# One attention layer inside a fused kernel: transposes alternate with attend products, a score product moves to the end of the step, normalising goes to three engines

## The reference

```python
scores = einsum('bqhd,bkhd->bhqk', q, k) / sqrt(32)      # 16 heads of 32
probs  = softmax(where(causal, scores, min))
attn   = einsum('bhqk,bkhd->bqhd', probs, v) @ Wo.T
mod    = 0.1 * tanh(attn @ A)
h      = rmsnorm(x, ln2_w)
gate   = silu(h @ W_in.T + mod * (h @ A) @ B)
out    = x + gate * (h @ W_up.T) @ W_down.T
```

## Time and profile before

| | us |
|---|---|
| median of 3 runs (1060.45 to 1062.85) | 1061.8 |
| the profiled execution | 1061.96 |
| its span | 1059.8 |
| PE busy | 1033.5 (98%) |
| DVE busy | 722.4 (68%) |
| ACT busy | 589.6 (56%) |
| POOL busy | 252.1 (24%) |

### The profile page before, as it was taken

The page is one execution under the profiler, slowest core; times in us unless marked ns, Lnnn a source line. Parts: engine busy times, 40 slices in busy tenths (PEclk is TensorE's granted clock), DMA queues, the critical chain, the costliest instruction groups (busy, mean ns, idle before and its releaser), DMA issues.

```text
span 1059.8 us, 17623 instructions
## 1 busy us (share of the span) xinstructions
PE 1033.5 (98%) x5336; PEld 853.5 (81%) x5337; DVE 722.4 (68%) x1661; ACT 589.6 (56%) x1399; POOL 252.1 (24%) x252
## 2 busy tenths in 40 slices
PE   6999999999999999999999999999999999999998
PEld 6787878877888878878888888778888888788887
DVE  7766756996665559985665479966655599854443
ACT  4464546886434447875444368864344478753342
POOL 4536123641000115640000136410001155300000
PEclk9999999999999999999999999999999999999999
DMA  6534133443222416343322354432234253322221
GB/s 239 201 141 161 49 117 74 96 110 134 90 89 91 147 47 173 69 127 129 106 90 89 111 141 98 113 130 90 89 91 147 63 157 80 95 86 89 89 89 50
DMA packets 47084, 115.93 MB, mean 109 GB/s; under 512 B 6800, under 2 KB 6800, under 8 KB 46096
## 3 DMA queue, kind: packets, MB, share of 16 engines
q1 hardware_dynamic: 43968, 105.06, 33.2%
q0 software_dynamic: 3040, 9.96, 2.7%
HBM read 76.46 MB, written 13.37 MB: 85 GB/s over the span
## 4 chain that ended last, share of the span: by engine, by line
PE 86%; DVE 8%; issue 3%; DMA 1%; ACT 1%; SPq 0%; DVEq 0%; POOL 0%; POOLq 0%
PE bank L518 67%; PE bank L721 5%; PE bank L735 4%; DVE wr L1329 3%; PE bank L684 3%; DVE nb L1341 2%; PE bank L688 1%; PE bank L770 1%; DMA stack<-wr 1%; PE bank L574 1%; PE bank L589 1%; DVE big L1350 1%; PE bank L632 1%; SPq L312 0%; ACT wr L887 0%
## 5 line engine op out<-in xcount | busy, mean ns | idle before, releaser
L518 PE MATMUL bank<-hT,wr 128*128 128x512 f32 x1488 | 358.4, 390 | 0.0
L518 PEld LDWEIGHTS bank<-hT,wr 128*128 128x128 f32 x1488 | 278.8, 188 | 60.0 <-issue 1.3
L518 PE MATMUL bank<-wr,actr 128*128 128x512 f32 (+1 forms) x1224 | 303.1, 397 | 2.4 <-DVE actr L1311 1.5
L518 PEld LDWEIGHTS bank<-wr,actr 128*128 128x128 f32 x1224 | 228.8, 190 | 51.1 <-issue 3.3
L491 POOL TENSOR_SCALAR big<-big,rr 128x128 f32<-128x128 f32 (+1 forms) x128 | 138.9, 1094 | 131.7 <-DVE rr L1346 131.2
L1380 DVE SCALAR_TENSOR_TENSOR wr<-stream,lns,wr 128x256 fp32r<-128x256 f32 x256 | 121.7, 536 | 51.0 <-ACT wr L1006 51.0
L972 ACT ACTIVATE big<-bank,nb 128x512 f32<-128x512 f32 (+3 forms) x256 | 131.7, 527 | 27.9 <-DVE nb L1341 27.7
L430 POOL TENSOR_TENSOR wqs<-wstage,wqs 128x512 fp32r<-128x512 f32 x32 | 43.0, 1353 | 436.8 <-ACT wqs L887 435.4
L1329 DVE TENSOR_TENSOR wr<-bank,wr 128x512 fp32r<-128x512 f32 (+1 forms) x224 | 124.5, 600 | 22.2 <-ACT wr L887 22.2
L887 ACT ACTIVATE wr<-bank 128x512 fp32r<-128x512 f32 (+1 forms) x224 | 106.0, 538 | 52.9 <-PE bank L518 30.1
L887 ACT ACTIVATE actr<-act_sb 128x512 fp32r<-128x512 f32 x64 | 40.4, 632 | 145.7 <-DVE act_sb L1394 145.7
(11 more groups left out here) (180 smaller groups left out, 1039.6 us busy)
## 6 DMA issues: line engine op xcount, KB each, us to landing
stream<-in_wmlp SPq DMA_DIRECT2D x64, 512.0 KB, 4.0
stack<-wr SPq DMA_DIRECT2D x192, 128.0 KB, 2.3
stream<-in_wmlp SPq DMA_DIRECT2D x64, 256.0 KB, 2.7
big<-in_x SPq DMA_DIRECT2D x4, 1024.0 KB
big<-y_rows SPq DMA_DIRECT2D x4, 1024.0 KB, 5.5
residual<-big SPq DMA_DIRECT2D x4, 1024.0 KB
big<-residual SPq DMA_DIRECT2D x4, 1024.0 KB, 5.6
out<-big SPq DMA_DIRECT2D x3, 1024.0 KB, 4.5
```

The costliest lines, as they stand in the source:

```text
L518: mm = pe.matmul(dst, lhs(pl, k), rhs(pr, k), start=start and i == 0, stop=stop and i == n - 1, skip_group_check=skip)
```

## The change

Four things change. The order of the transposes is kt 2, 1, 3, 0, and ACT and DVE take the banks as 6, 5, 4. The four transposes of kt 0 alternate with the attend products of kt 2 and kt 1 of the head before. Of the scores, row tile 3 of head n+4 is done at the end of step n, tiles 2 and 0 between the transposes, row tile 1 between the attends; the half projection of the next step moves to the end of the step, ahead of the score product. Normalising: row tile 3 on DVE, 0 on ACT (after its first bank copy), 1 and 2 on POOL, whose weights now come ahead of its scalings. The values banks change places.

```diff
-VALUES, LOW_RANK = (4, 6), 5
+VALUES, LOW_RANK = (6, 4), 5
-NORM_DVE, NORM_POOL = (3, 1), (0, 2)
+NORM_DVE, NORM_ACT, NORM_POOL = 3, 0, (1, 2)
+TURNED_BANKS = ((6, 256, 1024), (5, 512, 512), (4, 512, 0))
+PART_OF = {2: 1, 1: 2, 3: 2, 0: 3}
...
@@ POOL @@
                     for j in range(QH):
+                        if j < 2 and q < NQ - 2:
+                            weights_high(b, q + 2, j)
+                            weights_low(b, q + 2, j)
                         if q < NQ - 1 or j < QH - 1:
                             normalise((b * NQ + q) * QH + j + 1)
-                        if j < 2 and q < NQ - 2:
-                            weights_high(b, q + 2, j)
-                            weights_low(b, q + 2, j)
@@ PE @@
+            def scores_last(n, par, loads, first=False):
                 pe.wait_ge(stk[par], loads)
                 if not first:
                     pe.wait_ge(exp_ok, n * 4 - 3)
+                score_rows(par, 3, True)
                 mask(0, 3 * P, 1)
+            def scores_middle(n, par, first=False):
                 if not first:
                     pe.wait_ge(exp_ok, n * 4 - 1)
+                score_rows(par, 2, True)
+                score_rows(par, 0, False)
                 mask(1, 2 * P, 2)
+            def scores_second(n, par, first=False):
                 if not first:
                     pe.wait_ge(exp_ok, n * 4)
+                score_rows(par, 1, True)
                 mask(2, P, 1)
...
+            def turn_tiles(n, par, kt, first=False):
+                if not first and kt != 3:
+                    pe.wait_ge(pt_lo, (n - 1) * 3 + PART_OF[kt])
+                for qt in range(kt, TT):
+                    turn(n, par, kt, qt)
...
@@ PE, head_step: the new step @@
                 if head < H - 1:
+                    wait_probs(n + 1)
+                    for kt in (2, 1, 3):
+                        turn_tiles(n + 1, other, kt)
                 if head < H - 3:
+                    scores_middle(n + 3, other)
+                if head < H - 1:
+                    pe.wait_ge(pt_lo, n * 3 + 3)
+                    turn(n + 1, other, 0, 0)
+                    attend(2, HI)
+                    turn(n + 1, other, 0, 1)
+                    attend(2, LO)
+                    turn(n + 1, other, 0, 2)
+                    attend(1, HI)
+                    turn(n + 1, other, 0, 3)
+                    attend(1, LO)
...
+                if head < H - 3:
+                    scores_second(n + 3, other)
+                attend(3, HI)
+                attend(3, LO)
...
+                attend(0, HI)
+                attend(0, LO).then_inc(pv_done, 1)
+                if head < H - 1:
+                    project_part(b, head + 1)
...
                     up_part(0, head - UP_FROM)
+                if head < H - 4:
+                    scores_last(n + 4, j % 2, stack_loads(b, head + 4))
@@ PE, prelude @@
+                wait_probs(b * H)
                 pe.wait_ge(vpa_ok, b + 1)
+                turn_tiles(b * H, 0, 2, first=True)
                 pe.wait_ge(ha_ok, b + 1)
-                turn_probs(b * H, 0, first=True, values_out=b + 1)
-                scores(b * H + 2, 0, b * (H // 2) * 48 + 96)
+                turn_tiles(b * H, 0, 1, first=True)
+                turn_tiles(b * H, 0, 3, first=True)
+                pe.wait_ge(vpb_ok, b + 1)
+                turn_tiles(b * H, 0, 0, first=True)
+                scores(b * H + 2, 0, stack_loads(b, 2))
                 project(b, 1, 1, half=0)
+                project_part(b, 0)
+                scores_last(b * H + 3, 1, stack_loads(b, 3))
@@ ACT @@
+            def normalise(n, par):
+                act.wait_ge(rr_ok, n + 1)
+                rows = prob_rows(par, NORM_ACT)
+                a.activation(rows, rows, ACT.Copy, scale=rr[:, par, NORM_ACT:NORM_ACT + 1]).then_inc(pn_act, 1)
...
-                for i, (bk, w, at) in enumerate(((4, 512, 0), (5, 512, 512), (6, 256, 1024))):
+                for i, (bk, w, at) in enumerate(TURNED_BANKS):
                     act.wait_ge(p_turned, n * 3 + i + 1)
                     copy(pts[:, j % 2, HI, at:at + w], bank[bk][:, 0:w]).then_inc(pt_hi, 1)
+                    if i == 0 and (q < NQ - 1 or j < QH - 1):
+                        normalise(n + 1, (j + 1) % 2)
```

More of the change, by code:

```diff
@@ L676, in project, with score_rows @@
                     mm.then_inc(qk_done, 1)
-            def scores(n, par, loads, first=False):
-                pe.wait_ge(stk[par], loads)
[L681 to L689, removed]
+            def score_rows(par, qt, start):
+                bk, col, _ = SCORE[qt]
+                w = P * (qt + 1)
+                pe.matmul(bank[bk][:, col:col + w], stack[:, par, 0, qt * P:qt * P + P],
+                          stack[:, par, 1, 0:w], start=start, stop=False, skip_group_check=True)
@@ L692, in scores, with mask @@
+            def mask(bk, at, n):
+                pe.matmul(bank[bk][:, at:at + P * n], identr[:, :], maskr[:, 0:P * n],
+                          start=False, stop=True, skip_group_check=True).then_inc(s_done, 1)
+            def scores_last(n, par, loads, first=False):
+                pe.wait_ge(stk[par], loads)
                 if not first:
                     pe.wait_ge(exp_ok, n * 4 - 3)
-                rows(3, True)
+                score_rows(par, 3, True)
                 mask(0, 3 * P, 1)
+            def scores_middle(n, par, first=False):
@@ L726, in attend @@
[L726 to L737, removed]
@@ L739, in head_step, with scores, turn @@
-            def head_step(b, q, j):
-                n = (b * NQ + q) * QH + j
-                head = q * QH + j
+            def scores(n, par, loads, first=False):
+                scores_last(n, par, loads, first)
+                scores_middle(n, par, first)
+                scores_second(n, par, first)
+            def turn(n, par, kt, qt):
+                bk, col, _ = TURNED[kt]
+                src = SCORE[qt][2] + kt * P
+                mm = pe.transpose(bank[bk][:, col + (qt - kt) * P:col + (qt - kt) * P + P],
+                                  prob[par][:, src:src + P], ident[:, :])
+                if qt == TT - 1 and kt != 1:
+                    mm.then_inc(p_turned, 1)
@@ L745, in head_step, with project_part @@
+            def project_part(b, head):
+                q, j = head // QH, head % QH
                 if j == 0 and q < NQ - 1:
@@ L748, in head_step, with attend @@
                     project(b, q + 2, (0, 0, 1)[j - 1], half=(0, 1, 0)[j - 1])
+            def head_step(b, q, j):
+                n = (b * NQ + q) * QH + j
+                head, other = q * QH + j, (j + 1) % 2
+                def attend(kt, part):
+                    _, _, at = TURNED[kt]
+                    at_row = 64 * (j // 2) + R * (j % 2)
+                    return pe.matmul(bank[ATT][0:3 * R, kt * P:S], vst[:, q % 2, kt, at_row:at_row + 3 * R],
+                                     pts[:, j % 2, part, at:at + S - kt * P], start=False, stop=False,
+                                     skip_group_check=True)
+                if j == 0:
+                    pe.wait_ge(vst_lo, b * NQ + q + 1)
                 if head < H - 1:
-                    turn_probs(n + 1, (j + 1) % 2)
+                    wait_probs(n + 1)
+                    for kt in (2, 1, 3):
+                        turn_tiles(n + 1, other, kt)
                 if head < H - 3:
-                    m = b * (H // 2) + q * 2 + (j + 3) // 2
-                    scores(n + 3, (j + 1) % 2, m * 48 + 48)
-                attend(b, q, n, j)
+                    scores_middle(n + 3, other)
[9 more added lines that the diff above has]
+                    attend(1, LO)
+                else:
+                    pe.wait_ge(pt_lo, n * 3 + 1)
+                    attend(2, HI)
+                    attend(2, LO)
+                    pe.wait_ge(pt_lo, n * 3 + 2)
+                    attend(1, HI)
+                    attend(1, LO)
+                if head < H - 3:
+                    scores_second(n + 3, other)
+                attend(3, HI)
+                attend(3, LO)
+                if head == H - 1:
+                    pe.wait_ge(pt_lo, n * 3 + 3)
+                attend(0, HI)
+                attend(0, LO).then_inc(pv_done, 1)
+                if head < H - 1:
+                    project_part(b, head + 1)
                 if UP_FROM <= head < H - 1:
@@ L1054, in batch @@
                 split_qk(b, 1, 0)
+                normalise(b * H, 0)
                 for q in range(NQ):
```

45 lines of the change are left out of this document (17 added, 28 removed).

## The result

| | before | changed |
|---|---|---|
| median, 5 runs each | 1061.8 | 1070.55 (1068.07 to 1073.19) |
| ratio | | 1.0087, interval 1.0073 to 1.0101 |
| profiled execution | 1061.96 | 1073.19 |
| mean granted TensorE clock of its span | 0.998 | 0.994 |

A forecast was written before the change was run, and what follows sets the result against it. PE was taken to bound steps 0 to 7, DVE those from 9 on. Per batch +1.55 - 0.6 = +0.95, four batches +3.8: 1061.96 + 3.8 - 0.16 = 1065.6, range 1055 to 1071.

The forecast's parts named there:

- Alternation is worth 0: Transposes of kt 0 among attends: data movement (109 ns) sets their pace, not the 0.06 load, so alternating itself gains nothing.
- steps of 4.54: PE-bound head steps fall from 4.65 to 4.54, as two exposed weight loads of 0.05 each go.
- rival 1: Transposes are load-bound after all, so alternating makes kt 0's cost 57 ns each: 1059.2 in all; chance 12%.
- S3's waits: Row tile 3's score product waits for its stack DMA 0.9, 1.13 and 2.5 at steps 0, 4 and 8.
- The start of step 8: Per batch, prelude +0.22, early score product +0.29 and steps 0 to 7 put step 8's start 1.55 later.
- Steps 8 to 15: -0.6 a batch: From step 8 to the end of the last attend: 28.2 instead of 28.8, steps from 9 on 3.7 to 4.0.
- Normalising: On three engines: DVE's step falls to 3.7, ACT's scaling adds 0.3, POOL takes 2.33 instead of 2.17.
- DVE alone bound the late steps: In the kernel before, from step 9 on, DVE is the bound at 4.14 a step.
- rival 3: ACT becomes the bound through costlier normalising or late copies: +1.8 a batch, 1072.6; chance 15%.
- 2: Stack DMA arrives in time at the boundaries, no wait: -2.5 a batch, 1052; chance 20% together with its mild form.
- mild form: Late steps gain 1 more, ACT and DVE being ahead after step 8's wait: 1061; within the joint 20%.

The follow-up runs named there:

- e2: Changed kernel with the four kt 0 transposes in a row ahead of the four attends instead of alternating: 1066.46, ratio 1.0047 to the kernel before.
- e3: Changed kernel with eight added zero-weight products on PE at step 8, ahead of the score product that waits for the stack: 1068.26, ratio 1.0063.
- e4: Kernel before with only normalising on three engines (row tile 3 on DVE, 0 on ACT, 1 and 2 on POOL): 1059.35, ratio 0.9977.
- e6: Changed kernel with row tile 3's score product of each quarter's first head moved into the next step, and kt 0 transposes in a row: 1057.40, ratio 0.9958.
- e7: e6 plus head 2's first two score banks earlier in the prelude and step 0's values low-part wait only ahead of its attends: 1053.71, ratio 0.9922.

## Why the forecast was wrong, point by point

- **Alternation is worth 0; steps of 4.54.** Right: undisturbed steps took 4.51 to 4.55, and without alternation 4.50 to 4.53 (e2), so rival 1 is out. The Trainium skill's rule of columns/1.2 (TensorE: Matmul & The Clock Gate, section LDWEIGHTS (loading the stationary operand)), read for transposes, does not hold in these runs. A transpose's load took 0.06.
- **S3's waits.** Right at the boundaries: steps 4 of the first three batches took 5.66 to 5.70 against 5.67, and S3 at step 8 waits 2.2 to 2.3 in the idle list against 2.5; the twelve waits came, 13.8 in all against some 18. The start of step 8 moved by 223.32 - 179.37 less 221.71 - 179.40 = 1.64, forecast 1.55. That the two are so close is partly luck. The prelude grew by 0.92 (5.00 to 5.92), not by 0.51, because of the wait for the values' low part, which the forecast did not count; S3 at step 0 then waited 0.30 instead of 0.9, and step 0 took 5.13 instead of 5.44.
- **"Steps 8 to 15: -0.6 a batch."** This term failed twice. First, without any halved clock (e3) step starts after step 8 are 5.67, 9.51, 13.34, 17.40, 21.21, 25.08, the last attend 28.8, against 5.67, 9.44, 13.22, 17.21, 20.9, 24.75 and 28.2 forecast. So it is 0.0, not -0.6: about 0.3 on the way, of which POOL's pair (2.44, not 2.33) is a part and the rest is not traced, and 0.3 at the end, where I had counted two attends behind the last low part, though PE itself still had step 14's work and all eight attends of step 15 to do. That makes +1.65 a batch, 6.6 in all; e3 measured +6.4. Second, the clock, which is the next point.
- **The clock, which stood in no term.** I had 2.5 us of idle PE at step 8 in the forecast and priced only the wait. It brought half clock behind it in three of four batches of the profiled execution, 1.5 each; in the medians it is 2.3 (e3). The forecast's 3.8, with 0.4 for the start of step 8, 2.4 for the late steps and 2.3 for the clock, makes 8.9; measured is 8.75. (That 6.4 and 2.3 add up to it says nothing by itself, since both are differences to e3.)
- **Normalising.** ACT's scaling cost 0.41 recorded and 0.30 from its start to the next (180.94 to 181.24), as taken; POOL's 256 columns 1.18, taken as 1.09. ACT did not become the bound in the early steps. So rival 3 is out, though its 1072.6 lies nearer the measured time than the forecast: that nearness is chance. That DVE alone bound the late steps of the kernel before was wrong (e4), though the forecast's sum did not use it: it took the old steps as measured.
- **Rivals.** 2 was out (S3 did wait), and its mild form had the wrong sign: the late steps gained 0.6 a batch less than I had, not 1 more.

## What to carry to other kernels

A product moved ahead in an in-order queue takes its wait with it: add up how much work lay between the event that it needs and the product (here the product stood 5.7 us behind its step's start, 0.1 more than the DMA chain needed) and how much is left. Where TensorE will stand idle for 2 us or so, as here, count that half clock may follow it. Where a version loses, take its parts singly: here normalising on three engines gained 2.5 by itself, and the whole gained 4.5 (e6) once the stack's product kept its old distance to the DMA and the transposes of kt 0 stood in a row. When a wait moves to another place in its queue, as `vst_lo` did, ask what now stands behind it.

## What the runs showed of the hardware that was not expected

- A single idle stretch of 2.2 to 2.3 us in an otherwise full TensorE was followed by a stretch at 1.2 GHz in three batches and not in the fourth; with 1.8 to 2.0 us (e2) in one batch of four; with the idle cut to 0.3 to 0.5 (e3) in none.
- Transposes load their weights in 0.06 and move their 128 columns in 0.11, score products the other way round: loads 0.11, 128 columns 0.06.
- Behind a wait that ended late, PE's transposes started 0.44 after it in the three batches with computed wait values and 0.05 after it in the one with constants, four more waits lying between (0.1 each, an estimate).
- The same stack DMA (for the last head of a batch) landed 2.3 to 2.7 us after its third issue in all batches of the changed kernel and e3, and 3.9 to 4.5 in seven of the twelve batches of e2, e6 and e7; why stays open.
